# GpSimd's product with B released by the second product with C of the unit three back, in place of the first half scan of the unit two back

## What is computed

```python
dA = jnp.exp(dt[..., None] * A)
dBu = dt[..., None] * Bm[:, :, None, :] * u[..., None]
def step(h, inp):
    dA_t, dBu_t, C_t = inp
    h = dA_t * h + dBu_t
    y = jnp.einsum('bdn,bn->bd', h, C_t)
    return (h, y)
```

## Time and profile before

| | us |
|---|---|
| median of 3 runs | 1842.75 (1842.67 to 1843.38) |
| the profiled execution | 1843.9 |
| its span | 1842.1 |
| VectorE busy | 1361.4 (74%) |
| GpSimd busy | 1087.9 (59%) |
| TensorE busy | 1503.7 (82%) |
| ScalarE busy | 888.8 (48%) |

### The profile page before, as it was taken

How to read it: one execution, slowest core, us unless ns; L and a number is a source line. 1 busy time by engine, 2 the same in 40 slices (tenths; PEclk the granted TensorE clock), 3 DMA queues, 4 the chain that set the end, 5 groups by cost and what they waited for, 6 DMA issues and landing times. The chain is left out here.

```text
span 1842.1 us, 20793 instructions
## 1 busy us (share of the span) xinstructions
PE 1503.7 (82%) x5318; PEld 891.8 (48%) x5319; DVE 1361.4 (74%) x1532; ACT 888.8 (48%) x1962; POOL 1087.9 (59%) x636
## 2 busy tenths in 40 slices
PE   5867887889788788968887897897663899999997
PEld 3434444445344444534544453453342566666665
DVE  4389999999999998998999999999956122222222
ACT  2455645656474655656565565755521222222221
POOL 2375776776777678777767877667710233333332
PEclk8789898899899889988998998998885999999999
DMA  3403122231321223041213303123003634344332
GB/s 88 162 21 137 69 78 104 77 137 36 135 77 71 85 92 139 21 149 52 95 62 110 145 19 135 53 86 127 26 15 114 217 88 88 83 93 84 84 91 52
DMA packets 60432, 165.77 MB, mean 90 GB/s; under 512 B 17086, under 2 KB 29100, under 8 KB 60364
## 3 DMA queue, kind: packets, MB, share of 16 engines
q1 hardware_dynamic: 48220, 148.91, 23.5%
q0 software_dynamic: 12144, 16.13, 4.9%
HBM read 152.98 MB, written 12.03 MB: 90 GB/s over the span
## 5 line engine op out<-in xcount | busy, mean ns | idle before, releaser
L645 POOL TENSOR_TENSOR ring<-dtu,brep 128x1536 f32<-128x1536 f32 x192 | 669.0, 3487 | 273.5 <-DVE states L656 231.0
L668 PE MATMUL py<-ring,ident 128*128 128x384 f32 x1536 | 612.0, 547 | 204.3 <-ACT yg L681 130.3
L656 DVE TENSOR_TENSOR_SCAN states<-states,ring 128x768 f32<-128x768 f32 x384 | 673.7, 1755 | 46.9 <-ACT states L632 29.7
L668 PEld LDWEIGHTS py<-ring,ident 128*128 128x128 f32 x1536 | 309.7, 211 | 482.2 <-issue 143.4
L632 ACT ACTIVATE states<-dt_,aneg 128x376 f32<-128x376 f32 x768 | 406.2, 560 | 0.0
L658 DVE TENSOR_TENSOR ring<-states,crep 128x768 f32<-128x768 f32 x384 | 367.6, 957 | 13.2
L629 ACT ACTIVATE states<-zero_cols 128x16 f32<-128x16 f32 x384 | 70.7, 184 | 464.4 <-DVE ring L658 459.9
L1378 DVE COPY yidx<-place 128x1 int32 (+1 forms) x56 | 8.4, 154 | 245.7 <-DMA out_tokens<-ys,yidx 245.7
L1305 POOL DMA_INDIRECT xs<-x_scratch,yidx x56 | 55.4, 990 | 227.7 <-DVE yweight L1384 153.3
L1332 PE MATMUL gu<-w,xsT 128*128 x440 | 155.3, 496 | 5.0 <-issue 4.4
L467 PE MATMUL pf<-xT,wxz 97*128 97x384 f32 (+1 forms) x384 | 145.2, 517 | 7.6 <-ACT zs L482 4.9
(11 more groups left out here) (228 smaller groups left out, 1566.5 us busy)
## 6 DMA issues: line engine op xcount, KB each, us to landing
brep<-b_c_rows SPq DMA_DIRECT2D x64, 768.0 KB, 4.0
crep<-b_c_rows SPq DMA_DIRECT2D x64, 768.0 KB, 5.9
rest<-in_w_rest SPq DMA_DIRECT2D x55, 384.0 KB, 3.2
w<-in_w SPq DMA_DIRECT2D x8, 768.0 KB, 8.4
wd<-in_wd SPq DMA_DIRECT2D x8, 576.0 KB, 9.3
ptok<-in_p_tok SPq DMA_DIRECT2D x8, 384.0 KB, 4.0
pT<-in_p_T SPq DMA_DIRECT2D x8, 384.0 KB, 4.7
out_tokens<-h SPq DMA_DIRECT2D x8, 288.0 KB, 2.1
```

The source lines that it names most:

```text
L645: gp.tensor_tensor(ring[:, w % NRING], dtu[:, d, o, :].unsqueeze(1).to_broadcast([128, GN, T]), brep[:, ng], ALU.mult).then_inc(dbu_ok, 1)
L656: v.tensor_tensor_scan(h_in, h_in, x_in, 0.0, ALU.mult, ALU.add).then_inc(scan_ok, 1)
L668: mm = pe.matmul(py[:, 0:T], ident[:], ring[:, w % NRING, i, :], start=(ng == 0 and i == 0), stop=False)
```

## The change

One wait of GpSimd's product is on another semaphore. With U the unit of the product, it waited for 2 (U - 2) + 1 half scans; it now waits for 2 (U - 2) products with C, and the last of these is the second product of unit U - 3.

```diff
@@ pool_input @@
             wait(gp, y_ok, U + 1 - NRING)
-            wait(gp, scan_ok, 2 * (U - AHEAD) + 1)
+            wait(gp, hc_ok, 2 * (U - AHEAD))
             gp.tensor_tensor(ring[:, w % NRING], dtu[:, d, o, :].unsqueeze(1).to_broadcast([128, GN, T]), brep[:, ng], ALU.mult).then_inc(dbu_ok, 1)
```

## The result

| | before | after |
|---|---|---|
| median of 3 runs, us | 1842.75 | 1858.01 (1857.54 to 1861.98) |
| profiled execution, its span, us | 1843.9, 1842.1 | 1857.54, 1855.8 |
| VectorE busy, us | 1361.4 | 1380.2 |
| GpSimd busy, us | 1087.9 | 1082.4 |
| TensorE busy, us | 1503.7 | 1489.7 |

The ratio of after to before is 1.0088, with a 95% interval of 1.0065 to 1.0111: the change makes the kernel slower by 12 to 20 us. The medians are 15.3 us apart; 1853.6 had been forecast. VectorE, which sets the pace, is busy for 18.8 us more with the same instructions.

What follows compares the result with a forecast made beforehand. VectorE was taken as the bound throughout. Terms of -22.3 (step), +20.2 (embed), +2.0 (norm), +12.4 (reduce) and -1.5 (chunk starts) sum to +10.8, taking 1842.75 to 1853.6 us; own range 1849 to 1859, 8-in-10 range 1841 to 1864.

Steps and rivals of the forecast that it cites:

- What bounds the kernel: Whole kernel: VectorE sets the pace; GpSimd has about 2 us to spare per unit, VectorE waits for it only 8.9 us.
- which block the product meets: Between units: what counts is which VectorE block with two SBUF inputs GpSimd's product now meets, not how long GpSimd waits.
- The rival on L435: Unit 12's product, let go right behind L640, holds off the third L435: seven times 3.4 us more, 1877; chance 0.08.
- Step blocks: Chunks 1 to 7: unit 11's product no longer meets L591, nor L587 except in chunk 7; gain 22.3 us.
- Embed blocks: Seven places: unit 10's earlier product shuts out L396 for 2.8 us (four) or 3.0 us (three); loss 20.2 us.
- The rival of the short lines: Lines of 192 elements slip past a running product, so embed and norm losses vanish: 1831.3 us; chance 0.08.
- Norm block against L408: Rest of the embed block, six chunks: one L408 may wait up to 1.0 us for an L738; loss 2 us.
- Reduce blocks: Chunks 0, 1, 2 and 6: unit 5's product follows at once and holds L361 or L363 3.1 us; loss 12.4 us.
- the tails: Rival at reduce-block ends, chunks 3 to 5: the product beats L367 despite 0.2 us margin, 9.3 us more, 1862.9; chance 0.09.
- Starts of chunks: First product of a direction comes 0.5 us earlier, saving VectorE 0.5 us each in chunks 1, 2 and 6; gain 1.5 us.
- What its blocks lose reaches the end undiminished: Whole kernel: VectorE is the bound throughout, so the summed +10.8 us was to appear in full in the time.

## Why the prediction was right, and where it was off

*What bounds the kernel* and *which block the product meets*: right. VectorE's own lines grew by 18.8 us in sum, and its waits shrank by 3.4 up to the last unit.

That the time came out within 5 us of the forecast is partly luck. L435, a rival that is not in the sum, cost 9.6 us. Against it stand 6.6 us by which the other places came out lower than forecast, and 1.6 of these are the wait for TensorE in chunk 7. In the span the sum is 10.8 + 9.6 - 6.6 = 13.8, and 13.7 was measured; the medians, which are not of the profiled executions, lie 15.3 apart.

*Step blocks*, -22.3: -22.7 measured. Chunk 7 came as forecast, its product on L587 in place of L591:

```profile
1286.81 3.44 POOL L645 TENSOR_TENSOR ring<-dtu,brep 128x1536 f32<-128x1536 f32 x1
1287.20 4.26 DVE L587 SCALAR_TENSOR_TENSOR dt_<-dtu,dt_ 128x1152 f32<-128x1152 f32 x1
```

*Embed blocks*, +20.2: +20.0, with 3.05 to 3.07 where L396 follows without a gap (3.0 forecast) and 2.7 where it does not (2.8 forecast). The rival of the short lines fell: an instruction of 192 elements is held off like one of 1152.

*Norm block against L408*, +2: 0. L408's longest execution was 0.42. In chunk 4 ScalarE's L731 ended at 800.24, but L738 started only at 800.47, when the last L408 was under way (800.42 to 800.85):

```profile
800.04 0.20 ACT L731 ACTIVATE qrs<-qrs 128x3 f32<-128x3 f32 x1
800.47 3.17 POOL L738 TENSOR_SCALAR h<-h,qmv,qrs 128x192 f32<-128x192 f32 x3 [2.07 <-ACT qrs L731]
```

L738 itself took 3.17 for its three, against 3.00 in the earlier trace rows, so it was GpSimd that waited. I had put the hand-over from ScalarE at 0.1 us, and it is 0.23.

*Reduce blocks*, +12.4: +12.5, in the four chunks named. In chunks 3 to 5 the tails were not met.

*Starts of chunks*, -1.5: -2.2.

*The rival on L435* was given 0.08 and all seven places; it came true in three, for 9.6 us, and with unit 12 on the old release the time (1851.70) lies below the forecast and no longer above it. The step that failed is the count of 0.13 us by which the third L435 was to be ahead of the product. Chunk 1 after the change, where it is met:

```profile
329.65 4.83 DVE L435 TENSOR_SCALAR x_new<-h_new,hmv,hrs 128x192 f32<-128x192 f32 x3
329.81 1.06 POOL L640 TENSOR_TENSOR dtu<-dt_,u 128x384 f32<-128x384 f32 x1 [5.71 <-DVE dt_ L593]
330.95 3.42 POOL L645 TENSOR_TENSOR ring<-dtu,brep 128x1536 f32<-128x1536 f32 x1
```

and chunk 4, where it is not:

```profile
809.61 4.95 PE L668 MATMUL py<-ring,ident 128*128 128x384 f32 x8 [9.52 <-ACT yg L681]
...
812.16 0.96 DVE L658 TENSOR_TENSOR ring<-states,crep 128x768 f32<-128x768 f32 x1
...
815.69 2.74 PE L668 MATMUL py<-ring,ident 128*128 128x384 f32 x8
...
816.96 1.63 DVE L435 TENSOR_SCALAR x_new<-h_new,hmv,hrs 128x192 f32<-128x192 f32 x3
817.12 1.06 POOL L640 TENSOR_TENSOR dtu<-dt_,u 128x384 f32<-128x384 f32 x1 [5.80 <-DVE dt_ L593]
818.50 3.43 POOL L645 TENSOR_TENSOR ring<-dtu,brep 128x1536 f32<-128x1536 f32 x1 [0.31 <-PE py L668]
```

The product follows L640 by 0.08 us in chunk 1 (330.87 to 330.95). I had taken 0.17 from the earlier trace rows, and that row is from chunk 2, inside the loop, where the wait is held against a register. In chunks 0, 1, 6 and 7, which are written out, it is a constant, and the rows that belonged there were in the trace before: L640 ended at 105.99 and the product started at 106.07.

```profile
105.00 0.99 POOL L640 TENSOR_TENSOR dtu<-dt_,u 128x384 f32<-128x384 f32 x1
```

The third L435 starts 0.04 us after L640 has ended, in every chunk. With 0.08 it is recorded as starting 0.04 us ahead of the product, and that was not enough: in chunks 0, 1 and 6 it was held for 3.2 us all the same. In the loop (chunks 2 to 5) the product comes 0.31 us after L640, 0.27 behind the third L435, and L435 is spared; with no pacing wait at all it comes 0.24 after L640, and L435 is spared too. The 0.17 of the earlier trace rows does not hold here either. The profile puts the 0.31 down to TensorE in chunks 3 to 5, but that is a coincidence of times. The sum that ended at 818.43 is unit 9's, whose last product with C ended at 813.12; unit 8's sum, the one that is waited for, had ended at 814.56. In chunk 2 the product follows by the same 0.31. What the 0.31 us consist of stays open. In the loop of the changed kernel it is 0.31 to 0.33 for the first product of a direction and 0.17 for the product of unit 4.

*"What its blocks lose reaches the end undiminished"* was nearly so. At unit 19, where VectorE waits for ScalarE, the wait is shorter than before in chunks 1, 3 and 4 (by 0.7, 0.4 and 1.3 us) and longer in chunks 2 and 6 (by 0.6 and 1.0), 0.7 us given back in all. The end of chunk 7 is TensorE's and not VectorE's, and 1.6 us changed there.

## What to carry to other kernels

A wait that paces an engine with time to spare is not there for the time it costs; it decides what the engine runs beside. Before loosening one, list the instructions of the other engine that read all their tensor operands from SBUF (here lines with two such operands, and L435 and L367 with one), and see for each place whether the new release lies ahead of such a block or behind it. If there is a collision to be had for nothing, look for the work that caused it and move that (here 1.4%), and read hand-over times from the very place in the program in which they occur: here they differ between chunks that are written out and the loop, and within the loop from product to product.

## What was not expected of the hardware

- GpSimd's products and VectorE's lines with two tensor inputs in SBUF exclude each other for a whole instruction, and take turns: the one that waits goes next, even if the other's next instruction is already queued. In chunk 2 after the change three such turns stand in a row:

```profile
435.88 2.47 DVE L359 SCALAR_TENSOR_TENSOR resid<-turns,theta 128x768 f32<-128x768 f32 x1
437.50 4.17 POOL L645 TENSOR_TENSOR ring<-dtu,brep 128x1536 f32<-128x1536 f32 x1
438.39 4.10 DVE L361 SCALAR_TENSOR_TENSOR resid<-turns,resid 128x768 f32<-128x768 f32 x1
442.52 0.96 DVE L363 SCALAR_TENSOR_TENSOR resid<-turns,resid 128x768 f32<-128x768 f32 x1
```

- The shared thing is reading: a fill by GpSimd (128 x 1536 elements in 1.38 us) left a VectorE line with two SBUF inputs at 0.42 us, where a product held it for 3.1.
- A line with one tensor input in SBUF is held off just as long: L435 took 3.573 us in place of 0.374, and L367 3.455 in place of 0.356 in the one place in which it was met (chunk 0 without the pacing wait).
- A recorded start does not say who goes first when the two are close: the third L435 is recorded 0.04 us ahead of the product and was still held, three times of three; 0.20 and 0.27 us ahead it was not.
- GpSimd starts a product whose waits are already met 0.08 us after L640 in code that is written out, and 0.17 to 0.33 us after it inside the loop.
